# Moving steps between two chunks in the first phase of a Mamba, MoE and attention kernel

## The reference

```python
x = _layernorm(x + _L0_attn_ref(x, ...), axis=-1)   # Mamba-2, then the gated MLP
x = _layernorm(x + _L0_ffn_ref(x, ...), axis=-1)    # 8 dense experts, top 2 kept
x = _layernorm(x + _L1_attn_ref(x, ...), axis=-1)   # 16 heads of 8
x = _layernorm(x + _L1_ffn_ref(x, ...), axis=-1)    # 8 experts of capacity 512

# of the Mamba-2 mixer: u is the RMS-normed input, D_CONV = 4, D_STATE = 128
zxbcdt = u @ in_proj_w.T
xc = jax.lax.conv_general_dilated(xc, conv_w[:, None, :], (1,), [(D_CONV - 1, 0)], feature_group_count=CONV_DIM)
xBC = jax.nn.silu(jnp.transpose(xc + conv_b[None, :, None], (0, 2, 1)))
dBx = dt_t[..., None, None] * x_t[..., None] * B_t[:, None, None, :]
h = dA_t[:, :, None, None] * h + dBx                # one step of the scan over 1024 rows
y = jnp.einsum('bhpn,bn->bhp', h, C_t)
# of the gated MLP
mlp = jax.nn.silu(h @ gate_w.T) * (h @ up_w.T) @ down_w.T
# of the first experts
gate_logits = (jnp.einsum('bsd,ed->bse', x, Wg) + bg) / TEMP
topk_scores, topk_idx = jax.lax.top_k(gate_scores, K)
expert_outputs = jnp.einsum('bsd,eod->bseo', x, W) + b
# of the attention
xn = (x - mu) * jax.lax.rsqrt(var + LN_EPS) * ln_g + ln_b
qkv = (xn @ w_qkv + b_qkv).reshape(b, t, 3, H, hd)
```

## Time and profile before

| | us |
|---|---|
| median of three runs | 1392.61 (1388.61 to 1392.61) |
| the profiled execution | 1390.74 |
| its span, first to last instruction | 1389.0 |
| TensorE busy over the span | 1239.2 (89%) |
| VectorE busy | 1090.6 (79%) |
| ScalarE busy | 902.1 (65%) |
| GpSimd busy | 285.0 (21%) |

### The profile page before, as it was taken

One profiled execution on the slowest core, in us unless ns is written; L12 is line 12 of the kernel. 1 busy time (PEld: TensorE's weight loads), 2 busy tenths in 40 slices (PEclk: granted clock), 3 DMA queues, 4 the chain that ended last, 5 costly groups with the idle time before them and its releaser, 6 DMA issues. The chain is left out here.

```text
span 1389.0 us, 39431 instructions
## 1 busy us (share of the span) xinstructions
PE 1239.2 (89%) x16528; PEld 647.8 (47%) x16528; DVE 1090.6 (79%) x2184; ACT 902.1 (65%) x1739; POOL 285.0 (21%) x417
## 2 busy tenths in 40 slices
PE   5998888788887877999999999999999999994895
PEld 2556445453644522454555444444444544432462
DVE  6787787789676688899999989999999998944123
ACT  5665345437432302899998888888889988893242
POOL 2222131121112104200000110511104211034472
PEclk9999999999989988999999999999999999997998
DMA  5080000200113812111102211122102200011135
GB/s 141 1 230 16 1 2 16 108 2 1 61 49 74 152 68 109 44 38 44 43 17 62 52 45 35 46 68 54 43 18 56 62 22 18 18 34 46 45 108 188
DMA packets 59703, 77.72 MB, mean 56 GB/s; under 512 B 15010, under 2 KB 41189, under 8 KB 57686
## 3 DMA queue, kind: packets, MB, share of 16 engines
q1 hardware_dynamic: 56454, 70.95, 19.2%
q0 software_dynamic: 3072, 4.25, 1.0%
HBM read 37.18 MB, written 40.03 MB: 56 GB/s over the span
## 5 line engine op out<-in xcount | busy, mean ns | idle before, releaser
L1479 ACT ACTIVATE space<-ps 128x512 f32<-128x512 f32 x1024 | 605.2, 598 | 86.4 <-PE ps L667 37.2
L2139 DVE TENSOR_REDUCE smax<-ps 128x1 f32<-128x1024 f32 x512 | 613.3, 1220 | 51.1 <-PE ps L667 26.4
L667 PE MATMUL ps<-space 96*32 96x512 bf16 (+2 forms) x8432 | 609.9, 381 | 24.8 <-DVE smax L2139 13.8
L667 PEld LDWEIGHTS ps<-space 96*32 96x32 bf16 (+2 forms) x8432 | 251.4, 98 | 292.1 <-DVE smax L2139 44.2
L1047 PE MATMUL ps<-space 128*9 128x256 f32 x4096 | 315.8, 379 | 0.0
L1047 PEld LDWEIGHTS ps<-space 128*9 128x9 f32 x4096 | 116.2, 92 | 100.1 <-ACT space L1479 0.4
L1347 ACT ACTIVATE btok<-ps 128x128 f32<-128x128 f32 x32 | 8.9, 277 | 125.5 <-issue 101.5
L667 PE MATMUL ps<-w_exp,xnT 128*128 128x512 f32 x128 | 72.4, 694 | 14.4 <-DVE x L2084 14.4
L2084 DVE SCALAR_TENSOR_TENSOR x<-ps,gsel,x 128x128 f32<-128x128 f32 x256 | 69.1, 342 | 12.4 <-PE ps L667 12.1
L667 PE MATMUL ps<-ones,ident 128*128 128x512 bf16 x228 | 58.8, 418 | 17.4 <-POOLq L1695 12.3
L1949 DVE SCALAR_TENSOR_TENSOR space<-space,conv_w 128x512 f32<-128x512 f32 x96 | 71.2, 750 | 2.3
(11 more groups left out here) (250 smaller groups left out, 1375.4 us busy)
## 6 DMA issues: line engine op xcount, KB each, us to landing
head_sums<-space SPq DMA_DIRECT2D x31, 256.0 KB, 2.3
q_rows<-space SPq DMA_DIRECT2D x24, 256.0 KB, 2.4
k_rows<-space SPq DMA_DIRECT2D x24, 256.0 KB, 2.8
space<-k_rows SPq DMA_DIRECT2D x16, 384.0 KB, 5.4
space<-q_rows SPq DMA_DIRECT2D x16, 384.0 KB, 7.1
expert_out<-x_all SPq DMA_DIRECT2D x2, 2048.0 KB, 18.5
space<-expert_out SPq DMA_DIRECT2D x4, 1024.0 KB, 9.5
v_rows<-space SPq DMA_DIRECT2D x4, 576.0 KB, 3.3
```

What stands on the lines that cost most here:

```text
L667: return nc.tensor.matmul(out, lhsT, rhs, start=first, stop=last)
L1479: nc.scalar.activation(prob[:, QUAD * (step % PROB_SETS) + unit % QUAD, :], bank(STB + unit % 2), ACT.Exp)\
L2139: v.tensor_reduce(smax[:, N % 2, i:i + 1], ps[:, b0:b0 + 2, :].rearrange("p k n -> p (k n)"), AX.X, ALU.max).then_inc(S.s_max, 1)
```

## The change

Two changes of order are made together. No instruction is added or taken away, and no operand changes.

First, in slots with a tail (2 and 3 of those with a Mamba part), the last three convolution tiles move from rounds 4 to 6 to behind the rounds, on VectorE and, for their Silu, on ScalarE. The two halves of `tail_norm` are spread over rounds 4 and 5. The first half of the tail's rows is turned, and emptied by ScalarE, ahead of chunk 0's own steps; the second half stays behind them. `decays_so_far` goes ahead of `silu_conv` within a round.

Second, the experts' rows are turned one chunk later on TensorE (in chunk 1, behind that chunk's look-ahead), and emptied one chunk later on ScalarE. On VectorE several steps move in between `chunk_inputs` and `chunk_weights`: `normalise` in chunk 0, the two `cut_rest` (now in chunks 1 and 2 instead of 0 and 1), and the first `experts_scaled` of chunks 4 and 6.

```diff
+        def conv_in_mlp(q):
+            return N_CONV if q is None else N_CONV - 3
...
# TensorE
+                if q is not None:
...
+                    rows_turned_tail(q, 0)
                 if m is not None:
...
                     chunk_front(m, 0)
                     chunk_after(m, 0)
                 if q is not None:
-                    rows_turned_tail(q)
+                    rows_turned_tail(q, 1)
...
+                    if p is not None and c == 1:
+                        rows_turned_moe(p)
                     if p is not None and c == BIAS_AT:
                         gates_turned(p)
...
                     if p is not None:
-                        if c == 0:
-                            rows_turned_moe(p)
                         if c == 1:
                             route0(p)
# ScalarE
-                        if n >= 1:
-                            silu_conv(m, n - 1)
                         if n >= 2 * HID_TILES - 2:
                             decays_so_far(m, n + 2 - 2 * HID_TILES)
+                        if 1 <= n <= conv_in_mlp(q):
+                            silu_conv(m, n - 1)
                 if m is not None:
-                    silu_conv(m, N_CONV - 1)
+                    for j in range(min(conv_in_mlp(q), 2 * HID_TILES - 1), N_CONV):
+                        silu_conv(m, j)
                 table_of(ACT.Exp, 1)
+                if q is not None:
...
+                    evac_half("tail", q, 0, 7, scale=ln_g[:], bias=ln_b[:])
                 if m is not None:
                     chunk_copy(m, 0)
                 if q is not None:
-                    evac_T("tail", q, (7, 6), scale=ln_g[:], bias=ln_b[:])
+                    evac_half("tail", q, 1, 6, scale=ln_g[:], bias=ln_b[:])
...
-                    if p is not None and c == 0:
+                    if p is not None and c == 1:
                         evac_T("moe", p, (7, 5))
# VectorE
-                    if m is not None and 1 <= n <= N_CONV - 2:
+                    if m is not None and 2 <= n + 1 < conv_in_mlp(q):
                         convolve(m, n + 1)
-                    if q is not None and n == 4:
-                        for H in range(2):
-                            tail_norm(q, H)
+                    if q is not None and n in (4, 5):
+                        tail_norm(q, n - 4)
...
+                if m is not None:
+                    for j in range(conv_in_mlp(q), N_CONV):
+                        convolve(m, j)
...
                         chunk_inputs(m, c + 1)
+                    if p is not None and c == 0:
+                        for H in range(2):
+                            normalise(xa, x2, H, 0, 6 * p + H)
+                    if q is not None and p is not None and c in (1, 2):
+                        cut_rest(q, c - 1)
+                    if m is not None and p is not None and HT <= c < NT - 1:
+                        ahead = SCALED_AT[c][:1]
...
+                    for k in ahead:
+                        if c != BIAS_AT:
+                            experts_scaled(p, k)
+                    if m is not None and c < NT - 1:
                         chunk_weights(m, c + 1)
...
                     if p is not None:
-                        if c == 0:
-                            for H in range(2):
-                                normalise(xa, x2, H, 0, 6 * p + H)
...
-                    if q is not None and p is not None and c < 2:
-                        cut_rest(q, c)
```

More of the change, by code:

```diff
@@ L794, in mix_out, with rows_turned_tail @@
                 last.then_inc(S.mix_psum, 1)
-            def rows_turned_tail(b):
-                for H in range(2):
-                    pe.wait_ge(S.normed, 6 * b + 4 + H + 1)
-                    if b + 1 < B:
-                        pe.wait_ge(*((S.hid_ready, 2 * HID_TILES * (b + 2)), (S.skip_sum, 2 * (b + 2)))[H])
-                    else:
-                        pe.wait_ge(S.experts_used, 2 * E * (b + 1))
-                    transposes(lambda i: xn[:, H * HT + i, :], bank((7, 6)[H]), S.xT_psum)
+            def rows_turned_tail(b, H):
+                pe.wait_ge(S.normed, 6 * b + 4 + H + 1)
+                if b + 1 < B:
+                    pe.wait_ge(*((S.hid_ready, 2 * HID_TILES * (b + 2)), (S.skip_sum, 2 * (b + 2)))[H])
+                else:
+                    pe.wait_ge(S.experts_used, 2 * E * (b + 1))
+                transposes(lambda i: xn[:, H * HT + i, :], bank((7, 6)[H]), S.xT_psum)
             def qkv(b):
@@ L941, in _ @@
                     down(p, 1)
+                if q is not None:
+                    if p is None:
+                        score_pair(8)
+                        score_pair(9)
+                        keep_clock(OUTB, 24)
+                    rows_turned_tail(q, 0)
                 if m is not None:
@@ L1230, in xnT_free, with evac_half, evac_T @@
                     act.wait_ge(S.route_psum, B + b + 1)
-            def evac_T(kind, b, banks, **affine):
+            def evac_half(kind, b, H, at, **affine):
+                act.wait_ge(S.xT_psum, turned(kind, b) + H + 1)
+                func = ACT.Identity if affine else ACT.Copy
+                nc.scalar.activation(xnT[:, half(H)], bank(at), func, **affine).then_inc(S.xnT_ready, 1)
+            def evac_T(kind, b, banks):
                 xnT_free(kind, b)
                 for H in range(2):
-                    act.wait_ge(S.xT_psum, turned(kind, b) + H + 1)
-                    func = ACT.Identity if affine else ACT.Copy
-                    nc.scalar.activation(xnT[:, half(H)], bank(banks[H]), func, **affine).then_inc(S.xnT_ready, 1)
+                    evac_half(kind, b, H, banks[H])
             def input_squares(b):
@@ L2193, in _ @@
                         chunk_inputs(m, c + 1)
+                    if p is not None and c == 0:
[5 more added lines that the diff above has]
+                        ahead = SCALED_AT[c][:1]
+                    else:
+                        ahead = ()
+                    for k in ahead:
+                        if c != BIAS_AT:
+                            experts_scaled(p, k)
+                    if m is not None and c < NT - 1:
                         chunk_weights(m, c + 1)
@@ L2218, in _ @@
                         for k in SCALED_AT.get(c, ()):
-                            experts_scaled(p, k)
+                            if k not in ahead or c == BIAS_AT:
+                                experts_scaled(p, k)
                             if c == BIAS_AT:
```

11 lines of the change are left out of this document (4 added, 7 removed).

## The result

| us | before | after |
|---|---|---|
| median | 1390.61 (1388.59 to 1392.61, 4 runs) | 1365.70 (1362.29 to 1368.24, 4 runs) |
| ratio | | 0.9831 (95% interval 0.9807 to 0.9854) |
| profiled execution, its span | 1390.74, 1389.0 | 1364.65, 1362.9 |
| VectorE busy, TensorE busy | 1090.6, 1239.2 | 1091.9, 1224.1 |

The kernel is 24.9 faster by the medians and 26.1 by the profiled executions, where 21.4 were forecast. VectorE does nearly the same work (1.3 more); it waits less. TensorE's instructions are the same too, yet its busy time is 15.1 shorter (18.6 shorter in the first phase, 3.4 longer behind it): in the profiled executions its granted clock over slots 1 to 4 was 0.94, 0.93, 0.92 and 0.89 before and is 1.00, 0.96, 0.92 and 0.92 now, so less of it ran at half rate, the 1.2 GHz level.

What follows compares the result with a forecast made beforehand. No engine is full, so VectorE and TensorE must wait for each other in turn. 12.8 + 5.3 + 2.3 + 2.1 - 3.4 + 2.3 = 21.4 off 1390.7 gives 1369.3; 1361 to 1380 held some 0.85.

Steps and rivals of the forecast that it cites:

- Chunks 0 to 3, slots 2 and 3: `Gm` of chunk 1 to carry of chunk 3: fills cover VectorE's waits, 6.4 gained per slot, 12.8 in all.
- Slot 1: Chunks 0 to 3 without `cut_rest`: a new logits wait of 2.7 takes back the gain; 0.
- Chunks 4 and 6: Slots 1 to 3: eight scaled rows ahead of the weights cover the exponent's 0.88 at six places; 5.3 gained.
- Chunk 5: Pair product, slots 1 to 3: earlier scaled rows shorten TensorE's wait; one clock fall in three places assumed; 2.3 gained.
- Rounds and middle: Slots 2 and 3: 2.1 gained from the moved tiles and tail, 3.4 lost to a clock fall in both slots.
- Slot 4: No Mamba part: `cut_part` no longer behind the experts' rows, so the wait before `cut_rest` goes; 2.3 gained.
- The end: From slot 5's keys to the end: predicted 0.
- the signs named: Included slots 2 and 3 shorter by 8 to 10 each, slot 1 by 2 to 4, keys' wait near 3.
- the wait that moves: Slots 2 and 3: ScalarE's chain to the logits is longer, each keeps 2 to 3 of the 6.4; 1378, chance 0.15.
- the fall at every gap: The clock falls at both middles and all three pair products; 1374, chance 0.10.
- the open tiles: Slots 2 and 3: the three tiles lie open behind the rounds, 13.4 in two slots, so slower; 1395, chance 0.05.
- the rival in which the clock falls nowhere new: 4.7 gained at the pairs and no 3.4 lost in the middles, 27.2 in all; 1363.5, chance 0.10.

Runs made afterwards that it cites:

- the rounds' part alone: Only the rounds-and-middle half of the change (three tiles behind the rounds, tail's first half ahead of chunk 0), against the kernel before: 1389.53, ratio 1.0007.
- the rows early: The changed kernel with the experts' rows turned and emptied at chunk 0 again, VectorE's new order kept: 1368.45, ratio 0.9849 to the kernel before.
- the run without the early rows: The changed kernel with the scaled rows of chunks 4 and 6 behind the weights again: 1372.28, ratio 0.9883 to the kernel before.
- the fills late: The changed kernel with `normalise` and `cut_rest` behind the chunk's weights again, experts' rows still a chunk later: 1375.12, ratio 0.9911 to the kernel before.
- the run of slot 4 alone: The kernel before with the experts' rows turned and emptied at chunk 1 in slot 4 only, VectorE's order as before: 1384.52, ratio 0.9971.

## Why the prediction was right

**Chunks 0 to 3, slots 2 and 3** (12.8 predicted, 12.4 measured). The waits at the weights and at `cut_rest` went step by step as told: `normalise` covers the first exponent, the first `cut_rest` the second, the second `cut_rest` the third; the logits wait 0.94 (1.3 forecast); the shares and the carry don't wait. Three things in it were wrong or missing, and the total hides them. The carry's 1.22 was put down to the rows' transposes and the route, but what stood ahead of it was a pair at half rate; in the rounds' part alone, with the old order and the pair at full rate (1.88), the carry of chunk 3 doesn't wait. The later rows seem to spare that fall: the pair took 2.63 to 3.62 in 6 of 8 places with the rows early and over 1.88 in 1 of 18 with the rows late (2.35). Second, with the rows early again VectorE waits for the carry of chunk 1 (1.08) and not for the cut. Third, VectorE's work grew by 0.8 in each slot beside GpSimd, which the sum had at nothing, and the waits left were 0.6 less than the 1.5 forecast. That the two nearly cancel is luck.

**Slot 1** (0, measured 1.0). The logits wait 2.14 there and not 2.7, and the two waits that went, at the weights and the carry of chunk 1, were 1.69 and 1.68.

**Chunks 4 and 6** (5.3, measured 6.4, three times the 2.1 of slot 2). The sum took the shown wait of 0.88; with what goes along with it chunk 4 gave 1.19 each time and chunk 6 0.93.

**Chunk 5** (2.3, measured 4.0, what slots 1 and 3 gained over slot 2). One fall in three places was assumed, and none came. Chunk 5 itself is 2.57 shorter in each of slots 1 and 3, and 1.2 of that is lost again before the next slots begin. The step's reasoning (scaled rows earlier, TensorE still for a shorter time) is what the wait of 1.49 and the run without the early rows show, and the 24 places against 12 above.

**Rounds and middle** (2.1 and -3.4, measured -0.5). `hidden` 7 waits 1.94 and 1.68 (2.15 forecast); `Gm` of chunk 0 is 0.7 earlier in slot 2 and 0.8 later in slot 3 (0.9 and 0.6); the keys' wait at full clock is 3.11 ("near 3"). The fall of the clock came in one slot of two and cost 2.3 there; which slots it strikes changes from trace to trace (last section), so the -0.5 is this trace's. Without a fall each slot takes 35.3 (the rounds' part alone), together 1.8 less than before, near the 2.1 of the sum. That this half of the change is worth little was the sum's outcome, and the runs of each half show it.

**Slot 4** (2.3, measured 5.4) is the term that came out furthest off. The wait of 2.32 went, and 2.7 more came from the clock: three pairs at half rate in the trace before and one after. The prediction had no clock in this slot at all. Since the number of such pairs changes with the same order, the 2.7 is not shown to be the change's; run alone, the edit gave 4.0 (1.9 to 6.2), which fits 2.3 as well as 5.4.

**The end** (0, measured -2.6). From slot 5's keys on the order is the same and VectorE arrives 28.7 earlier; 26.1 is left at the end. From those keys to the end the thirteen traces, all with the same order there, take 848.0 to 851.8 (848.8 before, 851.5 in the changed kernel), so the 2.6 is within what executions differ by.

So the mechanism held, fills in front of VectorE's waits, and the nearness of the total owes something to luck: by slot 5's keys the traces are 28.7 apart, 7.3 more than the sum, mostly the clock's terms in chunk 5 and slot 4, and 2.6 of it went again at the end. Of the signs named, slot 2 is 10.0 shorter from `hidden` to `hidden` (8 to 10 forecast), slot 3 7.8 and slot 1 5.4 (2 to 4).

Of the rivals, the wait that moves (1378), the fall at every gap (1374) and the open tiles (1395) didn't come. The time lies between the forecast and the rival in which the clock falls nowhere new (1363.5). The rule that I weighed stands in the Trainium skill, page "TensorE: Matmul & The Clock Gate", section "HAM oscillation — how this bites in real kernels": a kernel whose matmul engine waits between its bursts starts each next burst at half rate, told there of waits of 3 to 5 us, longer than those here. It agrees with slot 3's gap (2.37, then 1.79 for two products) and not with slot 2's (2.37, then 1.02): in these traces a wait of 1.5 to 2.4 may or may not be followed by half rate.

## What to carry to other kernels

When two engines wait for each other in turn, list the waits that VectorE takes without a break behind them, and put work that is ready anyway in front of each: here a shown wait of 0.88 was worth 0.9 to 1.2 in chunks 3, 4 and 6, while in chunks 0 to 3 turning the rows later by itself gave less than half of what both gave. Look for the wait that takes the place of the old one (the logits, `hidden` 7) and fill that too: three tiles put behind the rounds alone gave nothing, and one of them moved back into the wait that they opened gave 5.9 by the medians, 5.0 by the ratios. And don't price a fall of the clock from one trace: look for the same order in the other traces first.

## What the hardware showed that was not expected

- TensorE's clock decides terms of 1 to 4 us each here, and the same gap in the same order doesn't always cost it. In five traces (the changed kernel, the rounds alone, the rows early, the fills late, the scaled rows late) the gap of 2.36 or 2.37 in front of the second half's transposes stands in slots 2 and 3; the two products behind it took 1.45 to 1.92 in six of the ten places and 1.02 in four. In slot 4 a pair behind 1.45 took 3.68 in the kernel before and 1.98 in the changed one, and a pair behind 1.83 kept 1.98 in the run of slot 4 alone, while one behind 1.55 took 3.01 before. The length of the one wait doesn't settle it; what does stays open.
- A wait costs more than the idle time that is shown: in chunk 4 1.19 for 0.88, since the instruction behind a wait doesn't overlap the one ahead (start to start 1.16 against 0.20) and hands over later (0.71 against 0.60).
- Work moved into VectorE's waits ran beside GpSimd's and both took longer: GpSimd's product of 128x256 3.41 for 0.61, VectorE's `normalise` 2.84 for 2.13. It cost VectorE 0.8 in each of slots 2 and 3; the cause was not tried.
